# A recurrence kernel: the sum of the second product with its projected tile, in the last pass, moved from VectorE to TensorE

## The reference

```python
def rms(z):
    return z / jnp.sqrt(jnp.mean(z * z, axis=-1, keepdims=True) + EPS)

O_lh = polar_orthogonal(W_lh)          # 12 iterations of X = 1.5 X - 0.5 X X^T X
O_rh = polar_orthogonal(W_rh)
q = jnp.einsum('btc,dc->btd', x, Wq)
v = jnp.einsum('btc,dc->btd', x, Wv)
def step(h, q_t):
    h_new = rms(h @ O_lh.T + q_t @ O_rh.T)
    return (h_new, h_new)
_, qs = jax.lax.scan(step, h0, jnp.swapaxes(q, 0, 1))
Y = jnp.einsum('btc,dc->btd', qs * v, Wc)
...
real = jnp.einsum('bti,io->bto', x, jnp.cos(theta + theta_noise))
imag = jnp.einsum('bti,io->bto', x, jnp.sin(phi + phi_noise))
return jnp.sqrt(real * real + imag * imag)
...
return x + attn(xn) + ffn(xn)
```

## Time and profile before

| what | value |
|---|---|
| median of 3 runs | 133.05 us (132.94 to 133.25) |
| the profiled execution, its own time | 133.2 us |
| its span, first to last instruction | 131.3 us |
| TensorE busy, share of the span | 112.1 us, 85% |
| VectorE busy | 85.1 us, 65% |
| ScalarE busy | 75.1 us, 57% |
| GpSimd busy | 68.4 us, 52% |
| mean granted TensorE clock | 0.985 |

### The profile page before, as it was taken

How to read it: one execution, slowest core, us unless ns; L and a number is a source line. 1 busy time by engine, 2 the same in 40 slices (tenths; PEclk the granted TensorE clock), 3 DMA queues, 4 the chain that set the end, 5 groups by cost and what they waited for, 6 DMA issues and landing times.

```text
span 131.3 us, 2507 instructions
## 1 busy us (share of the span) xinstructions
PE 112.1 (85%) x665; PEld 87.2 (66%) x665; DVE 85.1 (65%) x358; ACT 75.1 (57%) x283; POOL 68.4 (52%) x112
## 2 busy tenths in 40 slices
PE   6999999999868796989886969999999999987610
PEld 6888788878846474778664747676776666765300
DVE  3447777767666654555656647888788778878720
ACT  4164557585256574566846566766776776655100
POOL 6335889882367218011422225588888678874200
PEclk9999999999999999999999999999999999999985
DMA  4983000000000000000000000022020202202110
GB/s 105 282 309 124 2 0 7 0 0 5 0 0 0 0 0 2 0 0 5 0 0 0 0 0 5 5 82 77 3 80 0 80 0 82 79 8 80 40 45 10
DMA packets 3346, 4.98 MB, mean 38 GB/s; under 512 B 448, under 2 KB 1344, under 8 KB 3328
## 3 DMA queue, kind: packets, MB, share of 16 engines
q1 hardware_dynamic: 3024, 4.46, 9.9%
q0 software_dynamic: 160, 0.26, 0.6%
q10 hardware_dynamic: 144, 0.07, 0.2%
HBM read 2.69 MB, written 2.10 MB: 36 GB/s over the span
## 4 chain that ended last, share of the span: by engine, by line
PE 68%; DVE 17%; ACT 6%; issue 4%; DVEq 1%; ACTq 0%
PE bank L956 10%; PE bank L939 10%; PE bank L974 8%; PE bank L847 5%; PE bank L864 5%; PE bank L919 5%; DVE W L702 4%; PE bank L866 4%; PE bank L947 4%; PE bank L975 3%; DVE SQM L690 3%; DVE WMID L685 3%; PE bank L992 3%; DVE bank L696 2%; PE bank L805 2%
## 5 line engine op out<-in xcount | busy, mean ns | idle before, releaser
L302 POOL TENSOR_SCALAR XN<-X,MV,RSTD 128x128 f32<-128x128 f32 x32 | 25.6, 812 | 15.3 <-DVE RSTD L577 15.3
L309 POOL TENSOR_TENSOR FS<-FSQ 128x256 f32<-128x256 f32 x16 | 11.6, 727 | 13.5 <-ACT FSQ L460 13.5
L939 PE MATMUL bank<-CS,XNT 128*128 128x256 f32 x64 | 16.5, 380 | 0.0
L685 DVE SCALAR_TENSOR_TENSOR WMID<-UZ,RT,bank 128x129 f32<-128x129 f32 x29 | 10.1, 349 | 8.7 <-PE bank L974 4.3
L919 PE MATMUL bank<-IDENT,W 128*128 128x128 f32 x29 | 9.4, 323 | 7.4 <-DVE W L702 7.3
L956 PE MATMUL bank<-WCT,PV 128*128 128x128 f32 x64 | 14.8, 312 | 0.5 <-DVE OUT L720 0.4
L974 PE MATMUL bank<-PXT,WT 128*128 128x128 f32 x58 | 14.0, 323 | 1.2 <-DVE WT L669 1.1
L441 ACT ACTIVATE SQE<-W 128x129 f32<-128x129 f32 x30 | 9.4, 313 | 9.7 <-DVE W L702 9.7
L314 POOL TENSOR_TENSOR XF<-X,FR 128x256 f32<-128x256 f32 x16 | 11.6, 726 | 5.6 <-ACT FR L467 5.6
L919 PEld LDWEIGHTS bank<-IDENT,W 128*128 128x128 f32 x29 | 4.0, 139 | 14.7 <-DVE W L702 14.6
L669 DVE COPY WT<-bank 128x128 f32<-128x128 f32 x28 | 8.1, 291 | 8.5 <-PE bank L919 8.5
(11 more groups left out here) (169 smaller groups left out, 267.9 us busy)
## 6 DMA issues: line engine op xcount, KB each, us to landing
X<-in_L_attn_x_dram SPq DMA_DIRECT2D x8, 256.0 KB, 5.4
out_dram<-OUT SPq DMA_DIRECT2D x7, 256.0 KB, 2.0
out_dram<-OUT SPq DMA_DIRECT2D x2, 128.0 KB, 1.7
WP<-in_L_attn_W_rh_dram ACTq DMA_DIRECT2D x1, 64.0 KB, 2.0
WP<-in_L_attn_W_lh_dram SPq DMA_DIRECT2D x1, 64.0 KB, 2.2
ANG<-in_L_ffn_theta_dram POOLq DMA_DIRECT2D x1, 64.0 KB, 3.5
WV<-in_L_attn_Wv_dram SPq DMA_DIRECT2D x1, 64.0 KB, 3.3
ANG<-in_L_ffn_phi_dram POOLq DMA_DIRECT2D x1, 64.0 KB, 3.2
```

What stands on the lines that cost most here:

```text
L302: pool.tensor_scalar(XN[:, t, :], X[:, t, :], MV[:, t, 0:1], RSTD[:, t:t + 1], ALU.subtract, ALU.mult).then_inc(S["xn_done"], 1)
L309: pool.tensor_tensor(FS[:, f % 2, :, :], FSQ[:, f % 2, :, 0:P], FSQ[:, f % 2, :, P:2 * P], ALU.add).then_inc(S["ffn_sum"], 1)
L685: dve.scalar_tensor_tensor(out=WMID[:, 0:E], in0=UZ[:, uz(j), 0:E], scalar=norm_of(m), in1=YB[:, 0:E], op0=ALU.mult, op1=ALU.add).then_inc ...
L939: last = pe.matmul(FB[:, i * 2 * P:(i + 1) * 2 * P], XNT[:, tile(2 * f + i)], CS[:, :], start=True, stop=True)
```

## The change

In the last pass, `second` is left out of VectorE's program. ScalarE makes a tile SCALE instead, the identity times the norm of the state, right behind that norm, and TensorE adds SCALE x UZ to the second product in bank PB before it signals that product. VectorE's `end` waits for TensorE's signal in place of its own earlier sum. The first pass stays as it is.

```diff
+        SCALE = sb("SCALE", [P, P])
...
+            def norm_spread(m):
+
+                act.wait_ge(r_ready, m + 1)
+                act.activation(SCALE[:, :], IDENT[:, :], ACT.Copy, scale=norm_of(m)).then_inc(scale_ready, 1)
...
                 norm_of_state(m + 1)
+                if GUESSES <= m + 1 < LAST:
+                    norm_spread(m + 1)
                 if m in TILES_A:
                     xt_copied(TILES_A[m])
...
             def end(m, j):
-                dve.wait_ge(pre_ready, m + 1)
+                if m < GUESSES:
+                    dve.wait_ge(pre_ready, m + 1)
+                else:
+                    dve.wait_ge(y2_done, m + 1)
                 dve.wait_ge(rm_ready, m + 1)
...
                 mid(m, j)
-                second(m, j)
                 mid_transposed(m, j)
...
-                pe.matmul(PB[:, 0:P], stationary(m), O2T[:, :], start=True, stop=True).then_inc(y2_done, 1)
+                last = pe.matmul(PB[:, 0:P], stationary(m), O2T[:, :], start=True, stop=m < GUESSES)
+                if m >= GUESSES:
+                    pe.wait_ge(S["uz_copied"], min(m, len(PAIRS) - 1) + 1)
+                    pe.wait_ge(scale_ready, m - GUESSES + 1)
+                    last = pe.matmul(PB[:, 0:P], SCALE[:, :], UZ[:, uz(j) + 1, 0:P], start=False, stop=True)
+                last.then_inc(y2_done, 1)
```

More of the change, by code:

```diff
@@ L200, in bass_layer @@
         y1_done, y2_done, pre_ready = sem("y1_done"), sem("y2_done"), sem("pre_ready")
+        scale_ready = sem("scale_ready")
         mid_ready, ssm_ready, rm_ready = sem("mid_ready"), sem("ssm_ready"), sem("rm_ready")
```

## The result

The changed kernel takes 134.64 us (median of 6 runs, 133.98 to 135.22), the kernel before 133.15 in the same comparison (6 runs, 132.75 to 133.41): a ratio of 1.0112 with a 95% interval of 1.008 to 1.0145. It is slower, as forecast, but by 1.5 us and not by some 0.5, and 134.64 lies just outside the range of 133.15 to 134.6. The profiled execution took 134.66 us, 132.8 of it span; the one of before had 131.3.

The account below looks back on a forecast made before the run. The prediction took a loop of latencies, 2.87 us a move, as the bound. Adding 0.43 (move 14), 0.1 (fills) and 0 (removal, ffn moves) gave 133.6 us, 0.4% slower; 8-in-10 range 133.15 to 134.6.

Parts of the forecast that it names:

- What bounds the kernel: Each move is a loop of latencies through TensorE, VectorE, ScalarE and back, 2.87 us; TensorE is not the bound.
- What the removal saves: 16 VectorE sums of 0.35 us, 5.6 us busy time, worth nothing on the path; they become idle time before WTM.
- The ffn moves: Moves 15 to 26: SCALE (0.40) and its matmul are covered, cost 0; unfavourable end 0.05 each, 0.6 in all.
- Move 14: SCALE in front of the UZ copy on ScalarE is not covered and shifts everything after it by 0.43 us.
- The fills: Moves 27 to 29: SCALE's matmul pushes the transpose behind the fills, 0 to 0.27 us together, taken as 0.1.
- A: Rival: TensorE becomes the bound, ffn moves' transposes loaded over 0.13 late; about 134.9, or 136.6 to 137; chance 0.14.
- B: Rival: not slower, SCALE hides in ScalarE's shadow at move 14, shift 0.17; time 133.2; chance 0.16.
- C: Rival: faster, the removed sum held WTM; 15 moves give 3.6 less 0.5, about 130 us; chance 0.06.
- The sum: Whole program: +0.43 for move 14, +0.1 for the fills, +0 for the rest; 133.6 us, 0.4% slower.

Follow-up runs that it names:

- b: The kernel before with VectorE's `second` left out of the last pass, nothing in its place and no further passes run; 133.96 us, ratio 1.006.
- c: a_count_kept, but move 14 keeps VectorE's own sum and gets no SCALE; 133.37 us, ratio 1.0008 to the kernel before.
- h: a_count_kept without the four fill matmuls behind the second output matmul in moves 27 to 29; 134.31 us, one run.
- e_before_padded: The kernel before with 16 tiny VectorE memsets, 3 at the start and 13 in moves 6 to 12 of the first pass; 133.03 us, ratio 0.9986.
- d_count_shifted: The kernel before with 12 tiny VectorE memsets, two in each of moves 6 to 11 of the first pass; 133.95 us, ratio 1.0069.
- f: e_before_padded without the three fill matmuls in front of the transpose in moves 27 to 29; 132.97 us, ratio 0.9976 to the kernel before.
- g: a_count_kept without the three fill matmuls in front of the transpose in moves 27 to 29; 134.18 us, one run.
- a_count_kept: The changed kernel with one tiny VectorE memset in each last-pass move where the removed sum stood; 134.05 us, ratio 1.007 to the kernel before.

## Why the direction held and the size did not

- **What bounds the kernel: held.** A loop of latencies, 2.87 us, unmoved by 0.22 us more of TensorE's queue in each ffn move.
- **What the removal saves ("On the path they are worth nothing"): the step that failed.** It is true of the sum's duration, as b shows: WTM starts 0.77 behind `mid` with the sum or without it. But the step priced the removal at zero because the sum's time was hidden, and asked only what the sum does, not what it holds in its place. Removing 16 instructions moved two stops of VectorE from `second`, where the earlier trace rows's 0.16 of idle time took them up, onto W and the output step: 0.62 us in the trace, 0.67 in b's medians. It was to be seen in the trace of before: two moves of sixteen in which `second` comes 0.39 and 0.41 behind `mid` instead of 0.26. I read one move closely and took it for all.
- **The ffn moves: held.** 0 forecast for twelve moves, 0 found outside moves 17 and 26, and there b shows that it isn't SCALE. SCALE took 0.40 as forecast, and FSQ slid behind it (80.42, 0.30 after SCALE's start in move 15) without harm.
- **Move 14: held.** 0.43 forecast, 0.43 in the step (3.46 to 3.89), and gone with SCALE (c).
- **The fills: size held, way wrong.** 0.1 forecast, 0.11 between `mid` of 27 and of 29. The forecast let the transpose push W; h shows W on time and the delay on another way, through PV and the fills behind the output matmul.
- **The rivals.** A was not it: the transposes of the ffn moves are loaded 0.41 behind `mid`, 0.01 later than before. B was not: the UZ copy is 0.44 later. C was not, by b. What came was in none of them.
- **The sum.** 0.43 + 0.11 + 0.62 is 1.16 us, inside the measured interval (0.008 to 0.0145 of 133.15, 1.07 to 1.93) but 0.3 below its middle. Of that, one thing is to be seen: the profiled start-up was 0.32 later. Most of it is not the change's, for the same instruction, VectorE's first step on the norm, is 0.25 later in the changed kernel and as late in a kernel that has nothing of the change (timelines of before, after, e_before_padded, d_count_shifted):
```profile
5.17 0.17 DVE L523 TENSOR_SCALAR NRE<-NRM 128x2 f32<-128x2 f32 x1 [1.67 <-ACT NRM L360]
```
```profile
5.42 0.17 DVE L532 TENSOR_SCALAR NRE<-NRM 128x2 f32<-128x2 f32 x1 [1.98 <-ACT NRM L362]
```
```profile
5.43 0.17 DVE L526 TENSOR_SCALAR NRE<-NRM 128x2 f32<-128x2 f32 x1 [1.89 <-ACT NRM L361]
```
```profile
5.04 0.17 DVE L524 TENSOR_SCALAR NRE<-NRM 128x2 f32<-128x2 f32 x1 [1.50 <-ACT NRM L361]
```
What makes it early or late was not settled. The stretch behind the last `mid` varies as well, from 10.7 us (f, c) to 11.4 (g). The two timed kernels with SCALE in move 14 are 0.2 to 0.3 above what their steps add up to (after: 1.49 against 1.16; a: 0.76 against 0.54), and the single runs of g and h, which have it too, lie high as well (0.84 against 0.40, 0.97 against 0.32), while b, c, d, e and f agree to 0.1. Whether SCALE there costs more than the 0.43 in its step or these comparisons came out high stays open.

## What to carry to other kernels

An instruction that is hidden still has a place in its engine's list: before removing or adding some in a long unrolled kernel, look through all repetitions of the loop for single steps that are late with everything they need at hand, see whether they are a fixed count of instructions apart, and work out which instruction gets that number afterwards. If it is one on the path, a cheap instruction in an idle place moves the stop back (a_count_kept, e_before_padded). And in a loop of latencies ask of each signal who else hangs on it: in the fill moves the late tile did no harm where I looked, and its harm came through the engine that I had not followed.

## What the runs showed of the hardware

VectorE stood still for about 0.35 us at instructions 192, 320 and 448 of its list, counted from 0 with the waits: W of moves 17 (after, b: 0.70 behind WTM instead of 0.36) and of 16 and 24 (d: 0.70 and 0.72 instead of 0.35), the output step ahead of move 26 (after: 0.63 behind RINV instead of 0.26), `mid` of move 5 (before: 0.44 behind its copy, 0.09 in e). Four lists of different lengths put it at the same numbers, so that it goes with the count is shown. (In e the stop at 192 is not to be seen at all.) What stops the engine there stays open. The profile's table of DMA queues has two that carry instructions, here of the changed kernel (packets, MB, share):
```profile
q8 instruction: 7, 0.11, 0.3%
...
q14 instruction: 11, 0.09, 0.2%
```
So code is loaded while the kernel runs, in packets of about 8 KB on the second queue (0.09 MB / 11).

The traces also time these packets. In all ten kernels one of 8192 bytes starts on q14 0.63 to 0.95 us after the start of VectorE's instruction 320, and another so after that of 448 (before: `second` at 86.19 and the packet at 86.85, 109.14 and 109.78; d: W at 84.31 and the packet at 84.98). Where 192 is `mid` of move 5, in eight kernels, one starts 0.67 or 0.68 us after it; in e and f, where 192 is the reciprocal, 0.12 or 0.15 us after that. So a packet of code goes with each of the three places and moves with the count. But it starts when the late instruction is already running: what VectorE stands still for is not this packet. ScalarE shows the like in one place: in move 14 of the kernel before, FSQ starts 0.35 behind the start of the root, in move 20 0.11, and a packet starts 0.64 us later; no run was made on that.

The Trainium skill, page "Advanced Engine Details and Errata", section "ISA Cache", gives the cache for instructions lines of 16 KB, which it equates with 256 instructions, and says that this is configurable for each engine; an estimate from these figures is 64 bytes for an instruction, and 8 KB would be the 128 that lie between two stops here, half of the page's line. The page does not say that an engine stops at the end of a line. That both the stop and the load come from the end of a block is argued; no run here shows it.
